# A hybrid RWKV, feed-forward and attention kernel: tanh and u kept in PSUM, two constants as immediates, one step moved to GpSimd, one product saved in every second job, new orders

## The chip, the cores and the metric

The kernel runs on one core of a Trainium2 chip. The metric is the device time of one execution in microseconds. The profile is of one execution on the same core. Five engines work from queues of their own: PE (TensorE), DVE (VectorE), ACT (ScalarE), POOL (GpSimd) and SP (SyncE, which only issues DMAs here). Each takes its instructions strictly in the order in which they were written, and they wait for one another by semaphores.

## The reference, cut to what matters

Input x has 16 sequences of 512 tokens and 128 channels, all in fp32. Four blocks follow: `x + rwkv(norm(x))`, `x + ffn(norm(x))`, `x + attention(norm(x))` and `x + ffn(norm(x))`. The feed-forward quantises its operands blockwise to FP4. The change touches the first block, which has four layers; the part of a layer that matters is:

```
h  = layernorm(x);  hh = h shifted by one token
xk = h*tmk + hh*(1-tmk);  xv = h*tmv + hh*(1-tmv);  xr = h*tmr + hh*(1-tmr)
k, v, sr = xk@Wk, xv@Wv, sigmoid(xr@Wr)
x = x + (sr * wkv(time_decay, time_first, k, v)) @ Wo     # wkv: a scan over tokens
x = x + sigmoid(xr2@Wcr) * (square(relu(xk2@Wck)) @ Wcv)  # after a second layernorm and shift
```

## The kernel before, in words

A job is one layer of one sequence, 64 jobs r = 0 to 63, and each holds [128 channels, 512 tokens] tiles. The 16 sequences stay in SBUF (`X`). The work of a job is cut into some fifty steps, each a small function with an index. Every engine runs a loop over ticks t, and in a tick it issues its steps in an order written out by hand in the source, each for another job: `mul_u(t - 7)` is job t - 7's. So some thirteen jobs are in flight, and the text of the four loops sets the order on each engine. After job 63 the same loops carry 16 feed-forward jobs (`ffn_job`, from tick FFN_AT), 16 attention jobs (`att_job`, from ATT_AT) and 16 more feed-forward jobs (from FFN2_AT); the last steps of one kind run beside the first of the next.

In a recurrent job: norm1 (ACT, L757) and turn1 (PE, four transposes into bank bT) give h, which keep_h1 (ACT) writes to `h1` with the weight and bias of the norm. `sub_dh1` (POOL, L643) forms dh = h - hh. From job 10 on VectorE mixes xk and xr as dh*tm + hh (`mix_t` L307, `mix_rt` L314), and one product each gives k (bank bK) and r (bank bR). v takes two products into bank bV, `W*tmv` on h and `W2 = W*(1-tmv)` on hh (L1092, L1093). VectorE scans the running maximum of k (`scan_pp`), takes d = k - max (`sub_d`) and the capped argument d + time_first (`arg_r`, L337, into `er`). ScalarE forms the exponentials (`args`, `exp_r`, `exp_d`, `exp_k`); VectorE multiplies with v (`mul_rv` L344, `mul_s1` L351) and scans (`scan_bb` L358, `scan_aa` L366). GpSimd adds to the denominator and the numerator (`add_den`, `add_num`). The reciprocal is an approximation: `seeds` (ACT, L841, an exponential of the bits of the denominator), `mul_y` (POOL, L660, one per job), `square_1` (ACT, L848), `mul_u` (DVE, L373) and `rwkv` (DVE, L387); `gated` (DVE, L381) brings in tanh of r (`tanh_r`, ACT, L810) and `scaled_p` (POOL, L666) the seed. `seeds` and `square_1` read their additive constants from a two-column SBUF tile, `seed`. Then output (PE), `add_xa`, the second norm, `sub_dh` (POOL, L673), `mix_k` and `mix_r` (DVE, L404, L411), the four keys (L1135), relu and square (ACT, L867, L874), values (L1152), the gate product (L1142), `tanh_c`, `gate` and `add_xb` (POOL, L678). `rsqrts` (POOL, L601 to L606) takes the roots for the norms of two jobs at once.

The eight PSUM banks are handed from step to step: `bank.hand_over(semaphore, value)` says what ends the new use and returns what ended the last one, which the new user waits for. `lend_T`, `lend_O` and the like do it for a bank that another engine writes first. GpSimd has no access to PSUM in this kernel.

Of the kernel before, what the change touches and what calls it, by code (L numbers as in the profile page):

```python
# [7 lines left out]
I32 = mybir.dt.int32  # L8
ALU = mybir.AluOpType
# [22 lines left out]
FFN_AT = NR + 5  # L32
LN2_LAG = 6
EARLY = 10
GAP = 12
ATT_AT, FFN2_AT, TICKS = FFN_AT + NB, FFN_AT + NB + GAP, FFN_AT + 2 * NB + GAP + 18

# [38 lines left out]
def hybrid_program(nc, x_in, weights, vecs, rows, fp4w, qkv, wout, mask, ident, out):  # L76
    ctx = ExitStack()
    with ctx:
# [9 lines left out]
        class Norm:  # L88
# [30 lines left out]
        seed = sb("seed", [128, 2])  # L119
# [26 lines left out]
        lent_T, lent_O, lent_X, lent_Y, lent_M = {}, {}, {}, {}, {}  # L146
# [20 lines left out]
        consts, ew_done, wneg_done, omt_done, w_mixed, we_done = [sem(k) for k in (  # L167
            "consts", "ew", "wneg", "omt", "w_mixed", "we")]
# [34 lines left out]
        w2_of = lambda r: W2[:, r // NB, :]  # L203
        v_of = lambda r, k: vec[:, k, r // NB:r // NB + 1]
# [13 lines left out]
        def vector():  # L218
# [21 lines left out]
            def prepare_layer(l):  # L240
                wk = lambda k, n=1: W[:, l, k * 128:(k + n) * 128]
                w.wait_ge(w_here[l], 16)
                w.wait_ge(omt_done, 1)
                e.tensor_scalar(W2[:, l, :], wk(WV), omt[:, TMV - TMK, l:l + 1], None, ALU.mult).then_inc(w_mixed, 1)
                e.tensor_scalar(wk(WO), wk(WO), -0.5 * LEAD, None, ALU.mult).then_inc(w_mixed, 1)
                e.tensor_scalar(wk(WCV, 4), wk(WCV, 4), 0.5, None, ALU.mult).then_inc(w_mixed, 1)
                w.wait_ge(w_mixed, W_OPS * l + 1)
                e.tensor_scalar(wk(WV), wk(WV), vec[:, TMV, l:l + 1], None, ALU.mult).then_inc(w_mixed, 1)
                if l == 0:
                    for k, (matrix, mix) in enumerate(((WK, TMK), (WR, TMR))):  # L250
                        e.tensor_scalar(WE[:, 2 * k, :], wk(matrix), vec[:, mix, 0:1], None, ALU.mult)
                        e.tensor_scalar(WE[:, 2 * k + 1, :], wk(matrix), omt[:, mix - TMK, 0:1], None, ALU.mult).then_inc(we_done, 1)
# [79 lines left out]

            def arg_r(r):
                if 0 <= r < NR:
                    w.wait_ge(rwkv_done, r - 1)
                    w.wait_ge(d_done, r + 1)
                    e.tensor_scalar(er[r % 2][:, :], dd[r % 2][:, :], v_of(r, TF), CAP, ALU.add, ALU.min).then_inc(argr_done, 1)  # L337
# [31 lines left out]
            def mul_u(r):  # L369
                if 0 <= r < NR:  # L370
                    w.wait_ge(sq1_done, r + 1)
                    w.wait_ge(ps_done, r + 1)
                    e.scalar_tensor_tensor(out=p[r % 2][:, :], in0=pO[:, :], scalar=CUBIC, in1=p[r % 2][:, :],  # L373
                                           op0=ALU.add, op1=ALU.mult).then_inc(u_done, 1)

            def gated(r):
                if 0 <= r < NR:
                    w.wait_ge(rwkv_done, r - 1)
# [154 lines left out]
            for t in range(TICKS):  # L533
                fh_add(ffn_job(t - 7), 0)
                mix_rt(t - 6)
                mul_up(ffn_job(t - 6), 2)
                fh_sub(ffn_job(t - 7), 0)
                a_inverse(att_job(t - 7))
                arg_r(t - 6)
                weights_rounded(t - Q_AT - 2)  # L540
                fx_scale(ffn_job(t - 3))
                mix_r(t - 11)
                mul_up(ffn_job(t - 6), 3)
                fx_inverse(ffn_job(t - 3))
                init_affine(t - 2)
                mix_k(t - 10)
                fh_max(ffn_job(t - 6))
                fh_add(ffn_job(t - 7), 1)
                prepare(t - 4)
                fh_scale(ffn_job(t - 6))  # L550
                fh_sub(ffn_job(t - 7), 1)
                a_mask(att_job(t - 6), 0)
                gated(t - 7)
                a_max(att_job(t - 6), 0)
                fh_inverse(ffn_job(t - 6))
                mix_t(t - 5)
                weights_scales(t - Q_AT)
# [9 lines left out]
                a_mask(att_job(t - 6), 3)
                scan_aa(t - 6)
                bn1(t - 2)
                a_max(att_job(t - 6), 3)  # L570
                f_bn(ffn_job(t))
                a_bn(att_job(t))
                bn2(t - 8)
                mul_up(ffn_job(t - 5), 0)
                init_stats(t)
                gate(t - 12)
                scan_pp(t - 5)
# [6 lines left out]
                rwkv(t - 7)  # L584

        def gpsimd():
# [139 lines left out]
            for t in range(TICKS):  # L726
                add_num(t - 7)
                sub_dh(t - 10)
                rsqrts(t - 3)
                add_res(ffn_job(t))  # L730
                a_rsqrt(att_job(t - 2))
                fx_scaled(ffn_job(t - 4))
                init_rsqrt(t - 1)
                fx_divided(ffn_job(t - 3))
                scaled_p(t - 7)
                fh_scaled(ffn_job(t - 7), 0)
                mul_y(t - 7)
                add_xb(t - 13)
                weights_scaled(t - Q_AT - 6)
                sub_dh1(t - 4)  # L740
                fh_divided(ffn_job(t - 6), 0)
                fh_scaled(ffn_job(t - 7), 1)
                add_bias(att_job(t - 7))
                add_den(t - 6)
                fh_divided(ffn_job(t - 6), 1)
                f_rsqrt(ffn_job(t - 1))
                weights_divided(t - Q_AT)

        def scalar():
# [236 lines left out]
            for t in range(TICKS):  # L986
                silu(ffn_job(t - 6), 3)
                put_x(ffn_job(t - 9))
                tanh_c(t - 12)
                keep_hq(ffn_job(t - 8), 0)  # L990
                seeds(t - 7)
                fh_magic(ffn_job(t - 7), 1)
                keep_hq(ffn_job(t - 8), 1)
                relu(t - 11, 2)
                a_z(att_job(t - 3))
# [380 lines left out]
```

## Time and profile before

| | us |
|---|---|
| median of 3 runs (lowest, highest) | 1396.85 (1396.33, 1397.9) |
| span of the profiled execution | 1396.8 |
| PE busy | 1311.6 |
| ACT busy | 1261.8 |
| DVE busy | 1250.5 |
| POOL busy | 1160.8 |

The profiled execution's own time is its span, 1396.8 us; nothing stands around it in the table. Busy is the union of the instructions' times; instructions of one engine overlap at their ends, so an engine can look busy throughout and have its instructions start a fixed time apart that is shorter than the duration of each. The start of the next instruction less the start of this one is what it costs in a full queue. TensorE's granted clock is 0.9 or more of full speed in each of the 40 slices.

### The profile page before, as it was taken

What the parts mean: (1) busy time and instruction counts of PE and PEld (TensorE: products, weight loads), DVE (VectorE), ACT (ScalarE), POOL (GpSimd) and SP (SyncE); (2) the same over time, 40 slices, a digit from 0 to 9 for tenths busy, and PEclk for the clock granted to TensorE, in tenths of its full rate; (3) what the DMA queues carried; (4) which work ended last, traced back from release to release, by engine and by line L of the source; (5) the groups of instructions that cost most, each with busy time, mean ns of one, the idle gap of its engine ahead of it and who ended that gap; (6) DMA issues with size and microseconds to landing.
All of it is one profiled execution on the core that took longest, in us unless ns stands there. A gap on an engine that the chain in (4) does not pass through costs nothing.

```text
span 1396.8 us, 23610 instructions
## 1 busy us (share of the span) xinstructions
PE 1311.6 (94%) x7285; PEld 929.9 (67%) x7285; DVE 1250.5 (90%) x2169; ACT 1261.8 (90%) x2533; POOL 1160.8 (83%) x1218
## 2 busy tenths in 40 slices
PE   3699999999999999999999999999999999999997
PEld 1356667666666666676666677766667777667776
DVE  6999999999999999999999999579999467789994
ACT  6799999999999999999999999767777889888874
POOL 6888999999998999998998999969998445467983
PEclk9999999999999999999999999999999999999999
DMA  7000000000000000000000000100000000000011
GB/s 232 0 1 1 1 1 1 1 20 13 1 1 1 1 1 1 1 1 1 1 2 0 1 1 9 31 24 23 24 1 1 1 1 1 1 8 23 24 31 38
DMA packets 26924, 18.55 MB, mean 13 GB/s; under 512 B 1072, under 2 KB 26160, under 8 KB 26800
## 3 DMA queue, kind: packets, MB, share of 16 engines
q1 hardware_dynamic: 26800, 17.05, 4.2%
q8 instruction: 59, 0.97, 0.3%
q14 instruction: 65, 0.53, 0.1%
HBM read 12.85 MB, written 4.19 MB: 12 GB/s over the span
## 4 chain that ended last, share of the span: by engine, by line
ACT 40%; PE 30%; issue 11%; POOL 10%; DVE 8%; DMA 0%; ACTq 0%; SPq 0%; POOLq 0%; DVEq 0%
ACT z L757 10%; ACT kf L867 6%; PE ps L1211 5%; ACT kf L874 3%; PE ps L1190 3%; ACT rc L841 3%; PE ps L1152 3%; ACT ed L818 3%; PE ps L1183 3%; PE ps L1261 3%; PE ps L1135 3%; ACT er L835 2%; PE ps L1243 2%; ACT ed L819 2%; ACT ed L830 2%
## 5 line engine op out<-in xcount | busy, mean ns | idle before, releaser
L1152 PEld LDWEIGHTS ps<-W,kf 128*128 128x128 f32 x2048 | 245.9, 193 | 33.1 <-issue 32.3
L1135 PE MATMUL ps<-xk,W 128*128 128x512 f32 x512 | 262.5, 595 | 1.0 <-DVE xk L404 0.9
L1152 PE MATMUL ps<-W,kf 128*128 128x128 f32 x2048 | 251.2, 276 | 0.0
L757 ACT ACTIVATE z<-X,ln_rs 128x128 f32<-128x128 f32 x512 | 219.2, 720 | 6.1 <-POOL ln_rs L606 6.1
L867 ACT ACTIVATE kf<-ps 128x512 f32<-128x512 f32 x256 | 210.8, 823 | 3.5 <-PE ps L1135 3.5
L874 ACT ACTIVATE kf<-kf 128x1024 f32<-128x1024 f32 x128 | 164.7, 1287 | 0.0
L1040 PEld LDWEIGHTS ps<-idn,z 128*128 128x128 f32 x664 | 81.1, 143 | 113.7 <-issue 68.4
L1040 PE MATMUL ps<-idn,z 128*128 128x128 f32 x664 | 101.9, 277 | 32.8 <-ACT z L757 19.4
L604 POOL TENSOR_TENSOR ln_rs<-ln_rs,mhalf 128x8 f32<-128x8 f32 (+1 forms) x70 | 122.9, 1756 | 0.0
L707 POOL TENSOR_TENSOR W<-W,hsc 128x704 f32<-128x704 f32 x64 | 88.9, 1389 | 30.3 <-DVE hsc L482 30.3
L666 POOL TENSOR_TENSOR p<-p,rc 128x512 f32<-128x512 f32 x64 | 104.2, 1628 | 8.6 <-DVE p L381 8.0
L673 POOL TENSOR_TENSOR dh<-h 128x512 f32<-128x512 f32 x64 | 66.8, 1044 | 48.4 <-ACT h L860 48.2
L1190 PE MATMUL ps<-WU,d 128*128 128x352 f32 x256 | 99.9, 472 | 5.5 <-DVE W L463 4.8
L1183 PE MATMUL ps<-WG,d 128*128 128x352 f32 x256 | 97.6, 463 | 0.6 <-ACT d L898 0.6
L358 DVE TENSOR_TENSOR_SCAN bb<-ps,ed 128x512 f32<-128x512 f32 x64 | 78.3, 1223 | 19.5 <-ACT ed L830 19.4
L713 POOL TENSOR_TENSOR W<-W,hsc 128x704 f32<-128x704 f32 x64 | 88.8, 1388 | 2.6 <-DVE W L494 2.5
L226 DVE BATCH_NORM_STATS2 ln_st<-X 128x6 f32<-128x256 f32 x256 | 90.5, 413 | 0.1
L1122 PEld LDWEIGHTS ps<-W,rc 128*128 128x128 f32 x512 | 67.0, 191 | 33.8 <-issue 33.8
L1142 PEld LDWEIGHTS ps<-W,xc 128*128 128x128 f32 x512 | 64.3, 191 | 36.5 <-ACT sr L810 24.8
L649 POOL TENSOR_TENSOR er<-er,bb 128x512 f32<-128x512 f32 x64 | 81.4, 1273 | 2.3 <-DVE bb L358 2.3
L655 POOL TENSOR_TENSOR rv<-rv,aa 128x512 f32<-128x512 f32 x64 | 81.5, 1273 | 1.4 <-DVE aa L366 1.3
L678 POOL TENSOR_TENSOR X<-X,cr 128x512 f32<-128x512 f32 x64 | 81.5, 1273 | 0.0
(178 smaller groups left out, 4041.5 us busy)
## 6 DMA issues: line engine op xcount, KB each, us to landing
X<-x_in SPq DMA_DIRECT2D x16, 256.0 KB, 6.8
xi<-x_in SPq DMA_DIRECT2D x16, 256.0 KB, 2.8
out<-X SPq DMA_DIRECT2D x16, 256.0 KB, 2.3
W<-weights SPq DMA_DIRECT2D x4, 832.0 KB, 8.4
W<-fp4w SPq DMA_DIRECT2D x1, 560.0 KB, 3.6
row<-rows SPq DMA_DIRECT2D x1, 192.0 KB, 2.9
wqkv<-qkv SPq DMA_DIRECT2D x1, 96.0 KB, 5.9
idn<-ident SPq DMA_DIRECT2D x1, 64.0 KB, 3.0
```

The source lines that it names most:

```text
L226: last = e.bn_stats(g.of(g.st, n)[:, 2 * k:2 * k + 2, :].rearrange("p a s -> p (a s)"), src[:, k * 256:(k + 1) * 256].rearrange("p (a c) - ...
L604: e.tensor_tensor(rs[:, 0, :], rs[:, 2, :], mhalf[:, 0:k], ALU.pow).then_inc(*own.next())
L666: e.tensor_tensor(p[r % 2][:, :], p[r % 2][:, :], rc[r % 2][:, :], ALU.mult).then_inc(ps_done, 1)
L707: e.tensor_tensor(h, h, spread(hsc[n % 2][:, 0, k * 44:(k + 1) * 44], 44), ALU.mult).then_inc(fh_y[k], 1)
L757: last = e.activation(chunk(dst, j), chunk(src, j), ACT.Identity, bias=rs[:, 1, j:j + 1], scale=rs[:, 0, j:j + 1])
L867: e.activation(kf[r % 3][:, f, :], (pF0, pF1)[f % 2][:, :], ACT.Relu).then_inc(relu_done[f], 1)
L874: e.activation(both, both, ACT.Square).then_inc(sq_done[k], 1)
L1040: last = e.transpose(chunk(dst, j), chunk(src, j), idn[:, :])
L1135: e.matmul((pF0, pF1)[f % 2][:, :], w_of(r, WCK + f), xk[r % 2][:, :], start=True, stop=True).then_inc(kf_mm[f], 1)
L1152: last = e.matmul(chunk(pKV, j), kf[r % 3][:, f, j * 128:(j + 1) * 128], w_of(r, WCV + f), start=f == 0 and j == 0, stop=f == 3, skip_grou ...
L1183: e.matmul(pG[j % 2][:, 0:I], chunk(fx[n % 2], j), WG[:, :], start=True, stop=True).then_inc(g_mm, 1)
L1190: e.matmul(pU[j % 2][:, 0:I], chunk(fx[n % 2], j), WU[:, :], start=True, stop=True).then_inc(u_mm, 1)
```

## The change

- `tanh_r` writes its result to PSUM bank bV (over v, after `mul_s1` of that job) and no longer to an SBUF tile; `gated` reads it there. bV is handed to that use by a new `lend_V`. `mul_u` writes its result over bank bO and `rwkv` reads it there; bO stays in use until `rwkv`.
- The additive constants of `seeds` and `square_1` are immediates; the tile `seed` and its two memsets go.
- `arg_r` moves from VectorE to GpSimd, the instruction as it was.
- From layer 1 on (r >= 16), v of an odd job is mixed by VectorE (`mix_v`) and takes one product; of an even job it takes two still, on hh and dh. `big`'s third and fourth quarter hold the mixed tiles. The weights' preparation has one instruction less per layer from layer 1 on. `sub_dh1` and `keep_h1` wait for these uses of dh1 and h1.
- The order of the steps is written anew on all four engines. FFN_AT is NR + 6 (was NR + 5), ATT_AT is 85 as before, FFN2_AT is FFN_AT + 24 (was FFN_AT + 28). On GpSimd a tick's steps stand for earlier jobs than before (its loop runs about two ticks ahead of VectorE's).

```diff
-FFN_AT = NR + 5
-ATT_AT, FFN2_AT, TICKS = FFN_AT + NB, FFN_AT + NB + GAP, FFN_AT + 2 * NB + GAP + 18
+FFN_AT = NR + 6
+ATT_AT, FFN2_AT = FFN_AT + 15, FFN_AT + 24
+xv = [big[:, 2 + k, :] for k in range(2)]
+one_v = lambda r: r >= NB and r % 2 == 1
 def mix_rt(r):
-    w.wait_ge(p_done, r - 2)
+    w.wait_ge(r_mm, r - 2)
+def mix_v(r):
+    if 0 <= r < NR and one_v(r):
+        w.wait_ge(v_mm, r - 1)
+        w.wait_ge(dh1_done, r + 1 - EARLY)
+        e.scalar_tensor_tensor(out=xv[r % 2], in0=dh1[r % 2][:, :], scalar=v_of(r, TMV), in1=h1[r % 3][:, 0:T],
+                               op0=ALU.mult, op1=ALU.add).then_inc(xv_done, 1)
 def arg_r(r):        # moved from vector() to gpsimd()
     w.wait_ge(rwkv_done, r - 1)
     w.wait_ge(d_done, r + 1)
     e.tensor_scalar(er[r % 2][:, :], dd[r % 2][:, :], v_of(r, TF), CAP, ALU.add, ALU.min).then_inc(argr_done, 1)
 def mul_u(r):
-    e.scalar_tensor_tensor(out=p[r % 2][:, :], in0=pO[:, :], scalar=CUBIC, in1=p[r % 2][:, :],
+    e.scalar_tensor_tensor(out=pO[:, :], in0=pO[:, :], scalar=CUBIC, in1=p[r % 2][:, :],
 def gated(r):
-    w.wait_ge(rwkv_done, r - 1)
-    e.scalar_tensor_tensor(out=p[r % 2][:, :], in0=sr[r % 3][:, :], scalar=1.0, in1=rv[r % 2][:, :],
+    w.wait_ge(u_done, r - 1)
+    e.scalar_tensor_tensor(out=p[r % 2][:, :], in0=pV[:, :], scalar=1.0, in1=rv[r % 2][:, :],
 def rwkv(r):
-    e.scalar_tensor_tensor(out=rc[r % 2][:, :], in0=er[r % 2][:, :], scalar=2.0, in1=p[r % 2][:, :],
+    e.scalar_tensor_tensor(out=rc[r % 2][:, :], in0=er[r % 2][:, :], scalar=2.0, in1=pO[:, :],
 def tanh_r(r):
-    w.wait_ge(p_done, r - 2)
-    e.activation(sr[r % 3][:, :], pR[:, :], ACT.Tanh, scale=0.5).then_inc(sr_done, 1)
+    w.wait_ge(*lent_V[r])
+    e.activation(pV[:, :], pR[:, :], ACT.Tanh, scale=0.5).then_inc(sr_done, 1)
 def seeds(r):
-    e.activation(rc[r % 2][:, :], er[r % 2][:, :].bitcast(I32), ACT.Exp, bias=seed[:, 0:1],
+    e.activation(rc[r % 2][:, :], er[r % 2][:, :].bitcast(I32), ACT.Exp, bias=SEED,
 def square_1(r):
-    e.activation(pO[:, :], er[r % 2][:, :], ACT.Square, bias=seed[:, 1:2]).then_inc(sq1_done, 1)
+    e.activation(pO[:, :], er[r % 2][:, :], ACT.Square, bias=-1.0).then_inc(sq1_done, 1)
 def values(r):
+    if r < NB: ...               # as before: W on h1[1:], W2 on h1[:-1]
+    elif one_v(r):
+        w.wait_ge(xv_done, v_mixes(r + 1))
+        e.matmul(pV[:, :], w_of(r, WV), xv[r % 2], start=True, stop=True).then_inc(v_mm, 1)
+    else:
+        e.matmul(pV[:, :], w_of(r, WV), h1[r % 3][:, 0:T], start=True, stop=False)
+        e.matmul(pV[:, :], w2_of(r), dh1[r % 2][:, :], start=False, stop=True).then_inc(v_mm, 1)
+def lend_V(r):
+    lent_V[r] = bV.hand_over(p_done, r + 1)
```

The new orders, recurrent steps alone (other steps, between them, left out):

```
VectorE: scan_aa(t-6) scan_pp(t-5) bn2(t-8) mul_u(t-7) sub_d(t-5) rwkv(t-7) bn1(t-2) gated(t-6) mix_k(t-9)
         mix_t(t-4) mix_r(t-9) mix_rt(t-5) mix_v(t-4) gate(t-11) add_xa(t-7) mul_rv(t-5) mul_s1(t-5) scan_bb(t-5)
GpSimd:  sub_dh(t-11) arg_r(t-7) rsqrts(t-4) sub_dh1(t-5) mul_y(t-8) scaled_p(t-8) add_den(t-7) add_num(t-7)
         add_xb(t-13)
ScalarE: norm2(t-9) relu(t-10,0) square_1(t-7) tanh_r(t-6) square(t-11,1) keep_h2(t-9) relu(t-10,1) relu(t-10,2)
         square(t-10,0) seeds(t-6) args(t-5) keep_h1(t-3) exp_r(t-5) exp_k(t-5) exp_d(t-5) tanh_c(t-10)
         relu(t-10,3) norm1(t-2)
TensorE: turn1(t-4) ff_keys(t-11,3) lend_V(t-7) lend_T(t-6) output(t-8) values(t-6) lend_O(t-7) ff_keys(t-10,0)
         keys(t-5) receptance(t-6) ff_values(t-11,0) ff_keys(t-10,1) turn2(t-9) ff_keys(t-10,2) ff_gate(t-10)
         ff_values(t-11,1)
```

## Rows read from the trace of the kernel before

**Rows 1.** The page, part 1: busy time and share of the span.

```profile
PE 1311.6 (94%) x7285; PEld 929.9 (67%) x7285; DVE 1250.5 (90%) x2169; ACT 1261.8 (90%) x2533; POOL 1160.8 (83%) x1218
```

**Rows 2.** Table of windows (us from the start): length, busy us of each engine, clock, DMA.

```profile
190.00:700.00 510.00, 510.00 (x2783) 349.68 (x2782) 492.80 (x775) 510.00 (x968) 465.14 (x427) 1.00 0.01 3
700.00:780.00 80.00, 75.42 (x416) 52.31 (x415) 79.38 (x123) 76.77 (x146) 72.89 (x64) 1.00 0.00 1
...
850.00:950.00 100.00, 93.10 (x513) 69.47 (x512) 72.17 (x125) 77.14 (x150) 84.02 (x96) 0.93 0.09 25
...
1150.00:1250.00 100.00, 92.40 (x544) 68.23 (x543) 78.97 (x199) 90.49 (x220) 54.25 (x73) 1.00 0.00 1
1250.00:1350.00 100.00, 96.33 (x577) 72.67 (x576) 95.05 (x176) 81.28 (x170) 84.14 (x90) 1.00 0.09 27
```

The columns of rows 2 are PE, PEld, DVE, ACT, POOL, each busy us (and instructions).

**Rows 3.** Windows of single lines: L660, L1227 (two per attention job), L941 (one per feed-forward job).

```profile
318.00:450.00 132.00, 12.74 (x10) 1.00 0.00 1
...
1111.00:1149.40 38.40, 5.11 (x10) 1.90 (x10) 1.00 0.00 1
...
1280.00:1329.50 49.50, 2.99 (x5) 1.00 0.10 29
```

**Rows 4.** Waits of 190 to 700 us: waiter, released by; us, times, longest.

```profile
POOL dh L673 <- ACT h L860: 35.0, 39, 0.9
PEld ps L1142 <- ACT sr L810: 23.9, 39, 0.7
...
DVE bb L358 <- ACT ed L830: 15.5, 38, 0.4
```

**Rows 5.** Timeline of ScalarE: start us, duration us, line, instruction.

```profile
603.30 1.06 ACT L848 ACTIVATE ps<-er,seed 128x512 f32<-128x512 f32 x1
603.91 1.15 ACT L860 ACTIVATE h<-ps,vec 128x512 f32<-128x512 f32 x1
...
606.48 1.10 ACT L841 ACTIVATE rc<-er,seed 128x512 f32<-128x512 int32 x1
607.09 0.97 ACT L867 ACTIVATE kf<-ps 128x512 f32<-128x512 f32 x1
...
609.98 0.97 ACT L825 ACTIVATE ps<-ed 128x512 f32<-128x512 f32 x1
610.52 0.99 ACT L830 ACTIVATE ed<-ed 128x512 f32<-128x512 f32 x1
611.04 1.63 ACT L757 ACTIVATE z<-X,ln_rs 128x128 f32<-128x128 f32 x3
```

**Rows 6.** Timeline of TensorE's matmuls.

```profile
605.20 1.02 PE L1092 MATMUL ps<-h,W 128*128 128x512 f32 x2
606.06 1.02 PE L1093 MATMUL ps<-h,W 128*128 128x512 f32 x2
```

**Rows 7.** Timeline of VectorE.

```profile
606.07 0.74 DVE L387 SCALAR_TENSOR_TENSOR rc<-er,p 128x512 f32<-128x512 f32 x1
606.73 0.74 DVE L314 SCALAR_TENSOR_TENSOR sr<-dh,vec,h 128x512 f32<-128x512 f32 x1
607.39 0.47 DVE L337 TENSOR_SCALAR er<-d,vec 128x512 f32<-128x512 f32 x1
607.79 0.74 DVE L411 SCALAR_TENSOR_TENSOR xc<-dh,vec,h 128x512 f32<-128x512 f32 x1
...
609.72 0.74 DVE L307 SCALAR_TENSOR_TENSOR xt<-dh,vec,h 128x512 f32<-128x512 f32 x1
```

**Rows 8.** Timelines of GpSimd at four places, last the lines' table of 1150 to 1300.

```profile
609.87 1.73 POOL L666 TENSOR_TENSOR p<-p,rc 128x512 f32<-128x512 f32 x1
611.56 1.28 POOL L660 TENSOR_TENSOR er<-er,rc 128x512 f32<-128x512 f32 x1
...
813.00 1.27 POOL L666 TENSOR_TENSOR p<-p,rc 128x512 f32<-128x512 f32 x1
...
872.13 0.62 POOL L602 TENSOR_SCALAR ln_rs<-ln_st 128x4 f32<-128x4 f32 x1
...
888.33 0.23 POOL L602 TENSOR_SCALAR ff_rs<-ff_st 128x4 f32<-128x4 f32 x1
...
L694 POOL TENSOR_TENSOR z<-z,xsc 128x512 f32<-128x512 f32 x7 | 7.4, 1061 | 12.5 <-DVE xsc L442 12.5
```

More of the change, by code:

```diff
@@ L203, in hybrid_program @@
         w2_of = lambda r: W2[:, r // NB, :]
+        xv = [big[:, 2 + k, :] for k in range(2)]
+        one_v = lambda r: r >= NB and r % 2 == 1
+        v_mixes = lambda r: sum(one_v(k) for k in range(r))
         v_of = lambda r, k: vec[:, k, r // NB:r // NB + 1]
@@ L546, in vector @@
[L546 to L550, printed above, removed]
-                fh_sub(ffn_job(t - 7), 1)
[L552 to L557, printed above, removed]
+                fh_inverse(ffn_job(t - 6))
@@ L567, in vector @@
[L567 to L577, printed above, removed]
                 mul_u(t - 7)
                 sub_d(t - 5)
+                rwkv(t - 7)
+                bn1(t - 2)
+                gated(t - 6)
@@ L583, in vector @@
                 fx_sub(ffn_job(t - 3))
-                rwkv(t - 7)
+                mix_t(t - 4)
+                mix_r(t - 9)
+                a_inverse(att_job(t - 6))
+                fh_add(ffn_job(t - 6), 0)
+                mul_up(ffn_job(t - 5), 2)
+                mul_up(ffn_job(t - 5), 3)
+                weights_rounded(t - Q_AT - 3)
+                fh_sub(ffn_job(t - 6), 0)
+                fx_scale(ffn_job(t - 2))
+                a_mask(att_job(t - 5), 0)
+                prepare(t - 1)
+                fh_max(ffn_job(t - 5))
+                mix_rt(t - 5)
+                a_max(att_job(t - 5), 0)
+                fx_inverse(ffn_job(t - 2))
+                mix_v(t - 4)
+                fh_scale(ffn_job(t - 5))
+                gate(t - 11)
+                fh_add(ffn_job(t - 6), 1)
+                add_xa(t - 7)
+                mul_rv(t - 5)
+                mul_s1(t - 5)
+                scan_bb(t - 5)
         def gpsimd():
@@ L726, in gpsimd @@
             for t in range(TICKS):
-                add_num(t - 7)
[L728 to L737, printed above, removed]
-                add_xb(t - 13)
[L739 to L747, printed above, removed]
+                sub_dh(t - 11)
+                fh_divided(ffn_job(t - 8), 0)
+                fh_scaled(ffn_job(t - 9), 1)
+                a_rsqrt(att_job(t - 5))
+                arg_r(t - 7)
+                add_bias(att_job(t - 9))
+                rsqrts(t - 4)
+                add_res(ffn_job(t + 1))
+                init_rsqrt(t - 2)
+                fh_divided(ffn_job(t - 8), 1)
+                weights_scaled(t - Q_AT - 8)
+                f_rsqrt(ffn_job(t - 2))
+                fh_scaled(ffn_job(t - 8), 0)
+                fx_scaled(ffn_job(t - 5))
+                sub_dh1(t - 5)
+                weights_divided(t - Q_AT - 2)
+                mul_y(t - 8)
+                scaled_p(t - 8)
+                fx_divided(ffn_job(t - 4))
+                add_den(t - 7)
+                add_num(t - 7)
+                add_xb(t - 13)
         def scalar():
@@ L986, in scalar @@
             for t in range(TICKS):
[L987 to L995, printed above, removed]
                 silu(ffn_job(t - 5), 0)
-                args(t - 6)
+                keep_x(ffn_job(t - 9))
+                norm2(t - 9)
@@ L1025, in scalar @@
                 keep_h2(t - 9)
-                fx_magic(ffn_job(t - 3))
                 silu(ffn_job(t - 5), 1)
-                square(t - 11, 1)
-                fh_magic(ffn_job(t - 6), 0)
                 keep_fx(ffn_job(t - 4))
                 relu(t - 10, 1)
+                fh_magic(ffn_job(t - 6), 0)
                 silu(ffn_job(t - 5), 2)
+                relu(t - 10, 2)
+                square(t - 10, 0)
+                seeds(t - 6)
+                silu(ffn_job(t - 5), 3)
+                put_x(ffn_job(t - 8))
@@ L1034, in tensor @@
+                f_z(ffn_job(t - 1))
+                args(t - 5)
+                keep_h1(t - 3)
+                exp_r(t - 5)
+                exp_k(t - 5)
+                exp_d(t - 5)
+                a_z(att_job(t - 3))
+                keep_hq(ffn_job(t - 7), 0)
+                tanh_c(t - 10)
+                relu(t - 10, 3)
+                fh_magic(ffn_job(t - 6), 1)
+                norm1(t - 2)
+                keep_hq(ffn_job(t - 7), 1)
         def tensor():
```

194 lines of the change are left out of this document (96 added, 98 removed).

## The prediction

> **What bounds the kernel now.** The page comes first: on the whole span TensorE is busy 94%, and VectorE, ScalarE and GpSimd 90, 90 and 83% [rows 1]. No engine stands out, so I go by stretches. From 190 to 700 us, the recurrent stage with all its steps in flight, the table of windows has TensorE and ScalarE busy 510.0 of 510.0 us, VectorE 492.8, GpSimd 465.1 [rows 2]. Busy time there is a union of overlapping instructions and can hide small gaps, so I look for gaps in two other views. One job takes 13.2 us: the multiplication of L660, one per job, stands ten times in 132 us [rows 3]. The list of waits of that stretch has GpSimd waiting 0.9 us per job for h2, VectorE 0.4 us for the exponential, TensorE's weight loads for the tanh that frees bank bR (0.6 us of a load, of which most is covered by the matmul before it), and no entry for ScalarE at all [rows 4]. So ScalarE, in its written order, is packed for the whole stretch, TensorE is packed but for about 0.1 us, and both others have cover: 13.2 less 12.76 us of busy time on VectorE (492.8 / 38.6 jobs), 13.2 less 12.04 on GpSimd (465.1 / 38.6). An edit pays here only if it takes work from ScalarE, and TensorE has to give the same.
>
> **The change part by part.**
>
> *Two immediates.* In a packed queue the cost of an instruction is the time from its start to the next start. The two activations that read a bias column from `seed` cost 603.91 - 603.30 = 0.61 and 607.09 - 606.48 = 0.61 us; the 512-column exponential without a bias column, with the same kinds of source, costs 610.52 - 609.98 = 0.54 us when it writes PSUM, and the one after it 0.52 when it writes SBUF [rows 5]. I take 0.08 us for each, 0.16 us per job. ScalarE goes to 13.04 us. Bounds: 0 (the immediates cost what the column did) and 0.18.
>
> *Tanh into PSUM.* Same source, other destination. The exponential with an SBUF source costs 0.54 into PSUM and 0.52 into SBUF [rows 5]; I take 0, bounds -0.02 and +0.02 us per job. The wait it adds, on s1 of the job after (bank bV now holds tanh between `mul_s1` and `gated`), stands in ScalarE's queue ahead of square, keep_h2, relu and everything else. `mul_s1` of the next job is third from the end of VectorE's tick and tanh is fourth in ScalarE's next one, so nearly a fifth of a tick lies between, which I count as cover.
>
> *One product for v in every second job.* A 512-column product costs 606.06 - 605.20 = 0.86 us on TensorE, and v takes two of them [rows 6]. Of the jobs from 16 on, 24 save one: 20.6 us of TensorE's work in all, 0.43 us per job on the mean. The other jobs keep about 13.1 us (13.2 less the gap before ff_gate). So TensorE alternates between 13.1 and 12.2 us and stops being a bound. On its own this is worth nothing beyond 0.1 us per job, since ScalarE stands at 13.2; it is the cover under which the immediates count. VectorE pays for it with one mix, 607.39 - 606.73 = 0.66 us in every second job, 0.33 on the mean [rows 7].
>
> *VectorE.* It gives `arg_r` away, 607.79 - 607.39 = 0.40 us. `rwkv`, with both tensors in SBUF, costs 606.73 - 606.07 = 0.66; with one in PSUM I take 0.60, and nothing for `gated` [rows 7]. Sum: 12.76 - 0.40 - 0.06 + 0.33 = 12.63 us (12.96 in a job with the mix, 12.30 in one without). It stays under 13.04.
>
> *GpSimd takes arg_r.* No 512-column tensor_scalar on GpSimd stands in the trace. From below: at 4 columns it is 0.23 us (L602). From above: two full tensors at 512 cost 1.27 (L660). The nearest is the 512-column product with a small spread operand, 1.06 us (L694), and I take 1.04 [rows 8]. Against it stands what VectorE gives back. L666 costs 1.73 us where it starts beside VectorE's mix_t at 609.72 [rows 7], which reads two SBUF tensors, and 1.27 where it does not; L602 at 4 columns costs 0.62 at one place and 0.23 at another [rows 8], so the same instruction stretches there as well. In the new order the four or five mixes follow one another and GpSimd has `rsqrts` (small operands) about there, with scaled_p behind it beside a scan that reads PSUM. I expect L666 to come down by 0.45. Sum: 12.04 + 1.04 - 0.45 = 12.63 us, with the bounds 12.04 + 0.23 - 0.45 = 11.8 and 12.04 + 1.27 + 0.45 = 13.8 (arg_r itself held up beside mix_k, L666 as before). Under 13.04 at my value, over it from arg_r = 1.45 on.
>
> The Trainium skill (GPSIMD Engine Reference, 3.1) gives 769 ns for 512 elements in GpSimd's best one-input loop; with it GpSimd's sum would be 12.36 us. No run here shows it.
>
> *The orders.* I followed each semaphore through the four new lists with the costs above. Every wait is met at 13.04 us per job; the narrowest place is GpSimd's phase: `sub_dh` must start after keep_h2 (about 5.2 us into ScalarE's tick) and end before mix_k at 5.9 us into VectorE's, and its `rsqrts` must be done before norm1. That leaves some 0.5 us. The weight quantisation (its VectorE work stretched the ticks of 700 to 780 us, where ScalarE is busy 76.8 of 80 [rows 2]) is spread wider; I count 1 us gained, between -2 and 3. In the turn to the feed-forward jobs these start one tick later against a shorter recurrent tail; TensorE idles 6.9 of 100 us there now [rows 2]. I count 1 us lost, between 0 and 10 (a whole feed-forward tick). The second feed-forward pass starts 24 ticks after the first, before 28: attention-only ticks of 38.4 / 5 = 7.7 us go, and ticks of attention together with feed-forward come for them and for feed-forward ticks of 49.5 / 5 = 9.9 us [rows 3]. TensorE's work is the same, so only its idle time can be won, 7.6 us of 1150 to 1250 and 3.7 of 1250 to 1350 [rows 2]. I take 2 us won, between 8 lost and 8 won.
>
> *Sum.* 38.6 jobs of 190 to 700 us, the 5 after 780, some 5 before 190 and about half of the gain in the 6 disturbed ones make 52 jobs at 0.16 = 8.3 us. With 1 - 1 + 2 and another 1.2 us for TensorE's relief in the ticks in which it is late (the bounds: 0 and 3) it comes to 11.5 us. The profiled execution's span is 1396.8 us and the median of the runs 1396.85, so the two are taken as one: 1385.3 us.
>
> **The rivals.**
>
> *A, GpSimd becomes the bound and it turns slower.* For it: GpSimd is already the engine whose instructions stretch beside VectorE's two-input ones, and arg_r comes to stand right behind `sub_dh`, on which mix_k waits, so both start together. With arg_r held up by 0.45 and L666 not relieved, a job costs 12.04 + 1.27 + 0.45 = 13.76 on GpSimd; I price it at 13.44 (arg_r at 1.27, nothing given back): + 0.24 x 52 = 12.5, less the 3 us of the other terms: 1406 us. It decides from the point at which GpSimd's job passes 13.2 us. Against it: 0.9 us of idle time per job and the relief of two two-input instructions. Chance 0.13.
> The Trainium skill (SBUF — State Buffer, Terms) says that VectorE and GpSimd arbitrate for a shared port pair that is held for a full instruction while the loser fully blocks. By that rule GpSimd would lose the whole 3.0 us of the mixes; the rows above agree for L666 (0.45 lost beside one mix) and leave it open for L604.
>
> *B, the recurrent stage stays at 13.2 us.* The immediates cost what the column did, or GpSimd lands between 13.1 and 13.2. For it: only the start-to-start times of other functions speak for the 0.08. Then the edges alone remain: 1394 us. Chance 0.15.
>
> *C, the edges give more.* Second pass and turn win what idle time TensorE has, 8 to 10 us more: 1376 us. For it: 11.3 idle us in 1150 to 1350. Against it: a chain inside each job, not order, may make them. Chance 0.14.
>
> My forecast has 0.58.
>
> **How the numbers follow.** The forecast's own range is 1379 to 1391. C and B lie at 1376 and 1394, A at 1406; with half of A inside I reach 1371 to 1403. No change that can be told means within 0.2%, 2.8 us, so 1394.1 to 1399.6: half of B and a little of A, 0.08. Faster: 0.58 + 0.14 + half of B = 0.79. Slower: A and what the turn could lose, 0.13.
>
> **What would show it.** Right: the ten L660s in 127.6 to 130.4 us and no wait of ScalarE; square_1 and seeds at about 0.53 from start to start; TensorE with waits of 0.8 us in every second job; GpSimd at 12.6 busy us per job. Wrong: a wait of ScalarE for arg_r, or of mix_k for dh2 that grows from job to job (A); two activations still at 0.61 (B); the first pass of the feed-forward ending later than 1111 us by more than the recurrent stage won (the turn).

## The result and the profile after

The changed kernel takes 1431.0 us (median of 4 runs, 1429.38 to 1431.37) against 1396.88: a ratio of 1.0236, 95% interval 1.0222 to 1.0249. It is slower by 34 us where 1385.3 was forecast, and lies outside the range. The profiled execution's span is 1429.9 us.

The page's busy line of the changed kernel, and then its windows (PE, PEld, DVE, ACT, POOL as in rows 2):

```profile
PE 1315.8 (92%) x7237; PEld 923.8 (65%) x7237; DVE 1249.0 (87%) x2126; ACT 1266.2 (89%) x2539; POOL 1253.1 (88%) x1280
```

```profile
190.00:700.00 510.00, 489.53 (x2630) 330.90 (x2628) 476.15 (x720) 488.47 (x922) 497.52 (x444) 1.00 0.01 3
...
1345.00:1391.20 46.20, 46.20 (x284) 36.41 (x282) 46.09 (x80) 38.43 (x78) 40.15 (x38) 1.00 0.10 30
```

Against [rows 1] GpSimd has gained 92 us of work, no other engine more than 5. Against [rows 2] ScalarE and TensorE, full before, idle some 20 us in 190 to 700, and GpSimd has gone from 465.1 to 497.5. A job takes 138.4 / 10 = 13.84 us, read as in [rows 3] (the line of `mul_y` is L671 here):

```profile
289.90:428.30 138.40, 12.75 (x10) 1.00 0.03 9
```

The mean over jobs 16 to 48 is 13.84 too. GpSimd starts its `mul_y` alternately 14.03 and 13.65 us apart: the second instruction of the roots (L603) takes 0.63 us beside VectorE's mix of v, which comes in every second job, and 0.25 us without it. One of the longer jobs on GpSimd (start us, duration us), and L603 of the job after it:

```profile
601.53 1.28 POOL L671 TENSOR_TENSOR er<-er,rc 128x512 f32<-128x512 f32 x1
602.76 1.28 POOL L677 TENSOR_TENSOR p<-p,rc 128x512 f32<-128x512 f32 x1
...
607.68 1.08 POOL L684 TENSOR_TENSOR dh<-h 128x512 f32<-128x512 f32 x1
608.86 2.56 POOL L666 TENSOR_SCALAR er<-d,vec 128x512 f32<-128x512 f32 x1
611.49 0.53 POOL L602 TENSOR_SCALAR ln_rs<-ln_st 128x8 f32<-128x8 f32 x1
612.10 0.63 POOL L603 TENSOR_SCALAR ln_rs<-ln_st 128x8 f32<-128x8 f32 x1
612.70 1.66 POOL L605 TENSOR_TENSOR ln_rs<-ln_rs,mhalf 128x8 f32<-128x8 f32 x1
614.44 0.21 POOL L607 TENSOR_TENSOR ln_rs<-ln_rs 128x8 f32<-128x8 f32 x1
...
626.14 0.25 POOL L603 TENSOR_SCALAR ln_rs<-ln_st 128x8 f32<-128x8 f32 x1
```

`arg_r` (L666) costs 611.49 - 608.86 = 2.63 us. `scaled_p` (L677) takes 1.28 where it took 1.73 [rows 8]. There is no gap above 0.1 us; the small ones (ahead of L666 and inside the roots) add up to 0.34 us per job, which with 13.50 us of busy time fills the 13.84. So GpSimd is the full engine. What the others wait for has changed with it, against [rows 4]:

```profile
PEld ps L1056 <- DVE aa L369: 39.9, 35, 1.3
...
DVE xk L407 <- POOL dh L684: 31.5, 37, 0.9
```

```profile
ACT z L769 <- POOL ln_rs L607: 14.3, 37, 0.6
ACT er L850 <- POOL er L666: 7.2, 37, 0.2
```

mix_k waits for GpSimd 0.85 us in every job; GpSimd waited for ScalarE at that place before. ScalarE, which waited for nothing before, now waits for GpSimd's roots and for `arg_r`: 21.5 us, all that it idles in these 510 us.

On ScalarE the two activations with immediates, and tanh with PSUM as its destination:

```profile
604.19 0.58 ACT L863 ACTIVATE ps<-er 128x512 f32<-128x512 f32 x1
604.71 0.55 ACT L825 ACTIVATE ps<-ps 128x512 f32<-128x512 f32 x1
605.18 1.05 ACT L889 ACTIVATE kf<-kf 128x1024 f32<-128x1024 f32 x1
...
608.70 0.64 ACT L856 ACTIVATE rc<-er 128x512 f32<-128x512 int32 x1
609.22 0.73 ACT L833 ACTIVATE ed<-d,ew 128x512 f32<-128x512 f32 x1
```

0.52 us each from start to start (0.61 in [rows 5]), and 0.47 for tanh: the immediates did what they should.

Where the time lies is seen best by stage. The table is worked out from the starts of `mul_y` (job 0 is the first) and `keep_x` (feed-forward job 0 likewise) in the traces, in us:

| | to mul_y(15) | to mul_y(63) | to keep_x(0) | to keep_x(15) | to keep_x(31) |
|---|---|---|---|---|---|
| before | 241.9 | 635.0 | 82.7 | 151.2 | 283.1 |
| after | 255.7 | 666.5 | 79.5 | 151.9 | 273.4 |
| difference | +13.8 | +31.5 | -3.2 | +0.7 | -9.7 |

So the recurrent jobs lost 45 us and everything after them won 12. In the middle of the second feed-forward pass a job takes 46.2 / 5 = 9.24 us with TensorE busy 46.20 of 46.20 us (second window above), where it took 9.9 [rows 3] with VectorE as the full engine:

```profile
1280.00:1329.50 49.50, 48.06 (x283) 35.59 (x283) 49.50 (x91) 42.11 (x87) 45.50 (x51) 1.00 0.10 29
```

But only four jobs took 9.9 in the kernel before. Of the 9.7 us won in the last stage 5.8 lie before keep_x(21), in the stretch with the attention jobs, and 3.9 after it; experiment 7 comes back to this.

### The profile page after: what moved, and what is told of

Same layout as the page of the kernel before. It is cut to its first block, busy times and chain, and to the rows that moved or that the text cites. A ratio compares the mean times of both kernels' runs of the same rounds, so it can differ in the third digit from the quotient of the medians.

```text
span 1429.9 us, 23519 instructions
## 1 busy us (share of the span) xinstructions
PE 1315.8 (92%) x7237; PEld 923.8 (65%) x7237; DVE 1249.0 (87%) x2126; ACT 1266.2 (89%) x2539; POOL 1253.1 (88%) x1280
## 4 chain that ended last, share of the span: by engine, by line
PE 37%; POOL 21%; DVE 17%; ACT 15%; issue 9%; DMA 0%; POOLq 0%; SPq 0%; ACTq 0%; DVEq 0%
ACT z L769 7%; POOL er L666 6%; PE ps L1182 5%; PE ps L1241 5%; PE ps L1165 4%; POOL ln_rs L605 4%; PE ps L1220 3%; PE ps L1213 3%; DVE ln_st L228 3%; PE ps L1056 3%; POOL dh L684 2%; DVE aa L369 2%; PE ps L1229 2%; PE ps L1172 2%; PE ps L1152 2%
## 5 line engine op out<-in xcount | busy, mean ns | idle before, releaser
L1182 PE MATMUL ps<-W,kf 128*128 128x128 f32 x2048 | 256.8, 279 | 0.1
L769 ACT ACTIVATE z<-X,ln_rs 128x128 f32<-128x128 f32 x512 | 204.6, 482 | 35.0 <-POOL ln_rs L607 35.0
L666 POOL TENSOR_SCALAR er<-d,vec 128x512 f32<-128x512 f32 x64 | 157.7, 2463 | 8.7 <-DVE d L340 1.7
L1056 PEld LDWEIGHTS ps<-idn,z 128*128 128x128 f32 x664 | 76.9, 142 | 120.4 <-DVE aa L369 69.3
L882 ACT ACTIVATE kf<-ps 128x512 f32<-128x512 f32 x256 | 143.1, 586 | 3.8 <-PE ps L1165 3.8
L889 ACT ACTIVATE kf<-kf 128x1024 f32<-128x1024 f32 x128 | 135.0, 1055 | 0.0
L605 POOL TENSOR_TENSOR ln_rs<-ln_rs,mhalf 128x8 f32<-128x8 f32 (+1 forms) x70 | 115.0, 1643 | 0.0
L1165 PEld LDWEIGHTS ps<-xk,W 128*128 128x128 f32 x512 | 82.2, 190 | 30.7 <-issue 29.7
L228 DVE BATCH_NORM_STATS2 ln_st<-X 128x6 f32<-128x256 f32 x256 | 95.5, 413 | 0.1
L407 DVE SCALAR_TENSOR_TENSOR xk<-dh,vec,h 128x512 f32<-128x512 f32 x64 | 49.3, 770 | 52.6 <-POOL dh L684 52.6
L1220 PE MATMUL ps<-WU,d 128*128 128x352 f32 x256 | 92.9, 465 | 0.4 <-DVE W L466 0.4
L660 POOL TENSOR_TENSOR rv<-rv,aa 128x512 f32<-128x512 f32 x64 | 82.1, 1283 | 0.0
```

The costliest lines, as they stand in the source:

```text
L228: last = e.bn_stats(g.of(g.st, n)[:, 2 * k:2 * k + 2, :].rearrange("p a s -> p (a s)"), src[:, k * 256:(k + 1) * 256].rearrange("p (a c) - ...
L605: e.tensor_tensor(rs[:, 0, :], rs[:, 2, :], mhalf[:, 0:k], ALU.pow).then_inc(*own.next())
L769: last = e.activation(chunk(dst, j), chunk(src, j), ACT.Identity, bias=rs[:, 1, j:j + 1], scale=rs[:, 0, j:j + 1])
L882: e.activation(kf[r % 3][:, f, :], (pF0, pF1)[f % 2][:, :], ACT.Relu).then_inc(relu_done[f], 1)
L889: e.activation(both, both, ACT.Square).then_inc(sq_done[k], 1)
L1056: last = e.transpose(chunk(dst, j), chunk(src, j), idn[:, :])
```

## The experiments

Each median stands with its ratio to the kernel before, run on the same chip, and the 95% interval.

**1. arg_r back on VectorE, all else as changed.** Named A below.

```diff
 # gpsimd loop
-    arg_r(t - 7)
 # vector loop
     gated(t - 6)
+    arg_r(t - 5)
```

> The changed kernel with arg_r alone put back on VectorE, behind gated in the new order (job t - 5). Theory 1 (GpSimd is the bound, arg_r at 2.64 us from start to start is what fills it): GpSimd falls to about 11.2 us per job, VectorE rises from 12.4 to 12.8, and the job takes ScalarE's sum, 13.0 to 13.1 us instead of 13.87; over some 52 jobs that is 40 to 44 us less than the changed kernel: 1387 to 1391 us. Theory 2 (a chain through the new orders, sub_dh to mix_k to the next wait, sets the pace, whichever engine forms the argument): the job stays at 13.5 us or more, 1412 us or more, and the waits of mix_k for dh2 remain.

1376.1 us, 0.9848 (0.9834 to 0.9863). By stage 243.3, 625.3, 76.9, 151.9, 273.6. A ten-job window of `mul_y` and the table of 190 to 700:

```profile
190.00:700.00 510.00, 507.06 (x2778) 351.34 (x2777) 505.29 (x804) 510.00 (x982) 452.13 (x431) 1.00 0.01 3
```

```profile
300.70:430.90 130.20, 12.75 (x10) 1.00 0.03 10
```

ScalarE is full and a job takes 13.02 us (the mean over jobs 16 to 48 as well), as its sum says. One instruction's engine made 55 us: theory 1 in its mechanism, not in its size, as the time is 11 us below the lower end of what I expected. The recurrent stage before job 15 alone came back by 12.4 us, and my 52 jobs counted only a part of it.

**2. The kernel before with the immediates alone.**

```diff
-    bias=seed[:, 0:1]      # seeds
+    bias=SEED
-    bias=seed[:, 1:2]      # square_1
+    bias=-1.0
```

> The kernel before with the two constants as immediates and nothing else. Theory 1 (ScalarE and TensorE are both full at 13.2): ScalarE has 0.18 us less per job (the two cost 0.52 from start to start in the changed kernel, 0.61 before), TensorE keeps 13.1, so a job takes 13.1 us and the kernel gains at most 0.1 x 52 = 5 us: 1392 to 1395 us. Rival (ScalarE alone is the bound): 0.18 x 52 = 9 us, 1388 us. Rival (TensorE and the handing over of bank bR fix 13.2): no change, 1396 to 1397 us.

1391.35 us, 0.9955 (0.9940 to 0.9970). A job takes 13.10 us: the relief of ScalarE is cut off by TensorE's sum, 0.1 below.

**3. arg_r on GpSimd with one operation.** The time_first goes into the exponential as a bias column; the limit is a column, cap less time_first. The sum is formed in another place, so the output can differ by rounding.

```diff
-    e.tensor_scalar(er, dd, v_of(r, TF), CAP, ALU.add, ALU.min)
+    e.tensor_scalar(er, dd, col(lid, r), None, ALU.min)
-    e.activation(er, er, ACT.Exp)
+    e.activation(er, er, ACT.Exp, bias=v_of(r, TF))
```

> The changed kernel with GpSimd's arg_r cut to one operation: min with a column (cap less time_first, made once), and time_first added by ScalarE as the bias column of the exponential. If GpSimd's cost goes with the number of operations, arg_r costs 1.0 to 1.3 us instead of 2.56 and GpSimd stands at about 12.5 us per job; ScalarE pays 0.09 for the column (13.1): a job at 13.1, 1390 to 1394 us. If the cost is one of tensor_scalar on 512 columns as such, it stays at 2.0 to 2.6 us and the kernel at 1428 to 1434 us. Half way (1.8 us, GpSimd 13.2): 1395 to 1400 us.

1392.96 us, 0.9969 (0.9957 to 0.9982), 13.15 us per job. The instruction takes 1.57 us, half way, but the total lies in the range of the first case. The window of 190 to 700 and VectorE's wait for `sub_dh`:

```profile
190.00:700.00 510.00, 504.26 (x2749) 346.39 (x2748) 497.79 (x756) 509.56 (x971) 500.76 (x466) 1.00 0.01 3
```

```profile
DVE xk L409 <- POOL dh L687: 12.1, 20, 0.6
```

ScalarE is full again, and GpSimd has just come down to it: 500.76 / 38.8 = 12.91 busy us per job and 0.24 us of small gaps make the same 13.15, and mix_k still waits for it in every second job. One operation less was enough, with nothing to spare.

**4. GpSimd's forms by themselves.** Eight instructions ahead of the kernel before; their source is a tile filled for it. Only their durations are read, not the time (one run, 1411.62 us).

> The kernel before with eight GpSimd instructions of 512 columns put ahead of everything, one after the other, while VectorE has next to nothing to do; only their durations are of interest, not the time. Order: tensor_scalar with a column added and a constant minimum (arg_r's form); with two constants, add and min; a column added alone; minimum with a column alone; two constants, mult and add; a constant product alone; arg_r's form on 256 columns; tensor_tensor add with a column spread over 512. Theory 1a (the cost goes by operations): 2.0 us for the two-operation forms and near 1.0 for one, the 256-column one about half of the first. Rival 1b (the minimum has a slow path): forms 1, 2 and 4 near 2.0 and the others near 1.0. Rival 1c (the column operand costs): forms 1, 3 and 4 slow, 2, 5 and 6 fast. tensor_tensor as in the traces, 1.06 to 1.27.

GpSimd's timeline, in the order named there:

```profile
7.11 2.00 POOL L605 TENSOR_SCALAR kf<-kf,vec 128x512 f32<-128x512 f32 x1
9.20 1.92 POOL L606 TENSOR_SCALAR kf<-kf 128x512 f32<-128x512 f32 x1
11.22 1.57 POOL L607 TENSOR_SCALAR kf<-kf,vec 128x512 f32<-128x512 f32 x1
12.89 1.56 POOL L608 TENSOR_SCALAR kf<-kf,vec 128x512 f32<-128x512 f32 x1
14.54 0.63 POOL L609 TENSOR_SCALAR kf<-kf 128x512 f32<-128x512 f32 x1
15.26 1.51 POOL L610 TENSOR_SCALAR kf<-kf 128x512 f32<-128x512 f32 x1
16.87 1.15 POOL L611 TENSOR_SCALAR kf<-kf,vec 128x256 f32<-128x256 f32 x1
18.11 1.04 POOL L612 TENSOR_TENSOR kf<-kf,vec 128x512 f32<-128x512 f32 x1
```

None of the three theories as put. The minimum is no slower than the addition (1.56, 1.57), the column costs 0.05 to 0.1, one operation takes 1.5 and two take 1.9 to 2.0; arg_r's form on 256 columns takes 1.15, so an estimate from its two sizes is 3.3 ns per column and 0.3 us fixed. One form stands apart: two constants, a product and a sum, 0.63 us. That is the form of L601, the only two-operation tensor_scalar that GpSimd has in the kernel before. Adding the same column as a spread tensor (tensor_tensor) takes 1.04 us.

**5. A with two products for v in every job.**

```diff
-one_v = lambda r: r >= NB and r % 2 == 1
+one_v = lambda r: False
```

> The kernel with arg_r on VectorE (1376.1 us, a job 13.02 us from job 15 to 63) with v of every job from two products, mix_v gone. Theory (ScalarE's 13.0 is the bound and TensorE's 13.1 lies just above it): TensorE gets 20.6 us more in all, but a job goes only from 13.02 to 13.11 us, 0.1 x 48 = 5 us: 1380 to 1382 us. Rival (the one product is what won the time; TensorE is late in the disturbed ticks as well): 10 to 20 us, 1386 to 1396 us. Rival (the mix costs VectorE as much as the product gives): 1374 to 1377 us.

1380.75 us, 0.9886 (0.9869 to 0.9902); a job 13.10 us. As the theory has it: the saved product is worth 5 us, not its 20.6.

**6. A with the constants from the tile.** The edit is that of experiment 2, undone.

> The kernel with arg_r on VectorE, with the two constants read from the SBUF tile again. Theory: ScalarE's sum goes up by 2 x 0.09 = 0.18 us, a job from 13.02 to 13.20 us, 0.18 x 52 = 9 us: 1384 to 1386 us. Rival (ScalarE is not the bound in this kernel, the alternation of 12.2 and 13.9 us between jobs comes from VectorE and TensorE): 1376 to 1379 us.

1385.91 us, 0.9915 (0.9898 to 0.9931): + 9.8 us, theory. The immediates are worth more here than in experiment 2, because TensorE has been relieved.

**7. A with the second pass four ticks later.**

```diff
-ATT_AT, FFN2_AT = FFN_AT + 15, FFN_AT + 24
+ATT_AT, FFN2_AT = FFN_AT + 15, FFN_AT + 28
```

> The kernel with arg_r on VectorE, with the second feed-forward pass 28 ticks behind the first again, not 24. Theory (the closer start is what won about 10 us between the 16th and the last feed-forward job, 283.1 us in the kernel before, 273.6 here): 1384 to 1387 us. Rival (the new order inside the feed-forward ticks won it, 9.2 us per job instead of 9.9, and the closer start gave nothing): 1375 to 1379 us.

1377.1 us, 0.9852 (0.9838 to 0.9867), and keep_x(15) to keep_x(31) still 272.7 us. So the closer start won nothing, as the rival has it. But the rival's account of the 10.4 us against the kernel before (9.2 us a job for 9.9) is not what the trace shows: with the old start four feed-forward jobs of the second pass go at 9.89 us in the new orders too, VectorE busy 39.20 of 39.40 us. The 9.24 us in the changed kernel belong to the closer start, which puts more of the pass beside the attention jobs and wins nothing in sum. Of the 10.4 us, 6.5 come from the first three intervals of the pass (keep_x 13.49, 9.26 and 9.89 us apart; 16.93, 12.80 and 9.41 before), where it still meets the last attention jobs, 1.9 from two near its end, 0.8 from the stretch before its first keep_x and 1.1 from the eight intervals between. The new orders are the likely cause; the attention jobs also follow the first pass by 15 ticks here and by 16 before, and no run separates the two.

**8. A with tanh and u in SBUF, and tanh alone in SBUF.**

```diff
-    tanh_r: out=pV         gated: in0=pV           # both experiments
+    tanh_r: out=sr[r % 3]  gated: in0=sr[r % 3]
-    mul_u: out=pO          rwkv: in1=pO            # the first alone
+    mul_u: out=p[r % 2]    rwkv: in1=p[r % 2]
# cut: the waits and the handing over of bV and bO, as in the kernel before
```

> The kernel with arg_r on VectorE, with tanh and u written to SBUF tiles again and bV and bO handed over as in the kernel before. Theory (the move to PSUM takes 0.07 us from rwkv and otherwise frees GpSimd's reads beside it, none of which is on the bound): 1376 to 1378 us. Rival (VectorE, at 12.8 us per job and 13.2 in jobs with the mix, is a bound in every second job): 0.07 to 0.15 us per job, 1379 to 1384 us. Rival (holding bV and bO longer cost something): 1372 to 1375 us.

> The kernel with arg_r on VectorE (1376.1 us) with tanh alone in SBUF again; u stays in PSUM. With both back it took 1409.9 us, and there rwkv (both inputs in SBUF) took 1.44 us beside GpSimd's sub_dh instead of 0.67, while gated took its 0.67. Theory (a VectorE instruction with two SBUF inputs waits until the GpSimd instruction in flight is done, and rwkv is the one that meets one): u in PSUM is what counts, 1375 to 1379 us. Rival (bank bV's hand over or tanh's waits made the 34 us): 1400 to 1410 us.

Both in SBUF: 1409.94 us, 1.0090 (1.0075 to 1.0105), none of the three. Tanh alone: 1376.03 us, 0.9854 (0.9840 to 0.9869). So with tanh in SBUF, u's place makes all 34 us (u alone in SBUF was not run; bank bO is also handed over earlier with u in SBUF, which sets TensorE and ScalarE free sooner, not later). Where, is seen when VectorE's and GpSimd's timelines of the first are laid side by side:

```profile
604.93 0.67 DVE L382 SCALAR_TENSOR_TENSOR p<-ps,p 128x512 f32<-128x512 f32 x1
605.52 0.68 DVE L340 TENSOR_TENSOR d<-ps,pp 128x512 f32<-128x512 f32 x1
606.12 1.44 DVE L396 SCALAR_TENSOR_TENSOR rc<-er,p 128x512 f32<-128x512 f32 x1
607.49 0.75 DVE L228 BATCH_NORM_STATS2 ln_st<-X 128x6 f32<-128x256 f32 x2
```

```profile
605.96 1.05 POOL L685 TENSOR_TENSOR dh<-h 128x512 f32<-128x512 f32 x1
608.49 0.40 POOL L609 TENSOR_SCALAR ln_rs<-ln_st 128x8 f32<-128x8 f32 x1 [1.47 <-DVE ln_st L228]
```

`rwkv` (L396) with both tensors in SBUF begins at 606.12 beside GpSimd's L685, which ends at 607.01, and is done 0.55 us after that. With u in PSUM the median of that line is 0.67 us, here 1.43. With tanh alone in SBUF `gated` has two SBUF inputs, and in every second job it meets the same GpSimd instruction and stretches to 1.02 us likewise. That costs no time (1376.03 against 1376.1), though it uses up what VectorE had left: it is busy 509.43 of 510.00 us then, and ScalarE 509.42. One of these places:

```profile
600.74 1.00 DVE L390 SCALAR_TENSOR_TENSOR p<-sr,rv 128x512 f32<-128x512 f32 x1
```

```profile
600.16 1.04 POOL L685 TENSOR_TENSOR dh<-h 128x512 f32<-128x512 f32 x1 [0.82 <-ACT h L875]
```

In the first version VectorE becomes the full engine (510.00 of 510.00 us of 190 to 700) at 13.6 us a job, and GpSimd's roots come to wait for the statistics behind it. The Trainium skill (SBUF — State Buffer, Terms) has VectorE and GpSimd share a port pair that one of them holds for a full instruction while the other waits; here the trace agrees, for these two instructions (but see the last section).

**9. The kernel before, arg_r alone moved to GpSimd.**

```diff
 # gpsimd loop
     sub_dh(t - 10)
+    arg_r(t - 6)
```

> The kernel before, in its own orders, with arg_r alone moved to GpSimd, behind sub_dh (same job as before). Theory (the instruction's own 2.0 to 2.6 us is the whole cost, in whatever order): GpSimd's starts add up to 12.2 + 2.1 to 2.6 = 14.3 to 14.8 us per job instead of 13.2, over 52 jobs 57 to 83 us: 1454 to 1480 us. Rival (the new orders made it dear, by putting it beside the mixes): GpSimd hides most of it in its 0.9 us of idle time per job, below 1430 us.

1477.68 us, 1.0584 (1.0568 to 1.0600), 14.39 us a job, at the upper end of the theory. That the number fits is partly luck: the instruction takes 2.43 us, but it also waits 0.65 for rwkv of two jobs before, and `scaled_p` comes down to 1.27 us here as well, neither of which the theory had:

```profile
L654 POOL TENSOR_SCALAR er<-d,vec 128x512 f32<-128x512 f32 x28 | 68.1, 2432 | 18.3 <-DVE rc L381 18.3
```

The new orders did not make it dear: they took the 81 us that it costs in the old ones down to the 55 of experiment 1.

**10. The kernel before, tanh and u alone moved to PSUM.** The edit of experiment 8 the other way round, with `lend_V(t - 7)` ahead of `values(t - 6)`.

> The kernel before, in its own orders, with tanh and u in PSUM and nothing else. Theory (the old orders have no room for tanh in bV: values of the next job starts there at 618.4 us, gated reads at 622.3): TensorE's queue stands at values until gated is done, a job takes 14 to 16 us and the kernel 1440 to 1540 us. Rival (the phases of the engines shift and swallow it): 1395 to 1402 us. Rival (rwkv's relief shows at once): 1390 to 1395 us.

1749.96 us, 1.2538 (1.2517 to 1.2559), 18.8 us a job, beyond the theory's upper end, by its mechanism and one turn more. Waits of 300 to 700 us:

```profile
DVE rv L344 <- ACT er L835: 109.3, 21, 5.5
ACT h L803 <- PE ps L1041: 107.3, 21, 5.4
PEld ps L1093 <- DVE p L381: 83.6, 21, 4.0
PE ps L1093 <- DVE p L381: 66.3, 21, 3.2
```

TensorE stands at values for gated; turn1, behind it in TensorE's queue, is late for keep_h1; exp_r, behind that in ScalarE's, is late for mul_rv; and gated comes after that in the next tick. A ring through three queues (TensorE, ScalarE, VectorE), not a sum of one engine. The granted clock is 0.87 in that stretch, in which TensorE is busy 333.7 of 400 us; before it was 1.00.

**11. A with all feed-forward and attention jobs one tick earlier.**

```diff
-FFN_AT = NR + 6
+FFN_AT = NR + 5
```

> The kernel with arg_r on VectorE, all feed-forward and attention jobs one tick earlier (FFN_AT = NR + 5, as before). Theory (the turn's idle time shrinks by part of a tick): 1370 to 1376 us. Rival (TensorE's work is the same there, and a recurrent tick just gets longer): 1375 to 1378 us. Rival (a wait on the last recurrent jobs stops a queue): 1380 us or more.

1383.26 us, 0.9907 (0.9892 to 0.9921): 7 us slower than A. Of the profile's 7.4 us to the last keep_x, 3.7 lie before job 63, 2.6 between it and keep_x(0), and 1.7 after keep_x(15). The time lies in the range of the third case; whether its mechanism is at work has not been followed further. The planned tick was the better one.

## Why the prediction was wrong, point by point

- *What bounds the kernel.* Right: ScalarE full, TensorE 0.1 us below. With ScalarE relieved alone a job takes TensorE's 13.10 us (experiment 2, and experiment 5 in the new orders), and with TensorE relieved alone ScalarE's 13.20 (experiment 6).
- *Two immediates.* Right, 0.09 each against 0.08. Worth 6 us alone and 9.8 with TensorE relieved.
- *One product.* Right: cover, not a gain. 5 us, with 20.6 taken from TensorE.
- *GpSimd takes arg_r.* This step failed, and with it the sign. I took 1.04 us and gave 1.27 as the upper end; it costs 2.00 us alone (experiment 4), 2.56 beside VectorE's mixes. The upper end was no bound. The 0.23 us of L602 at 4 columns says nothing of the cost per column, and two-tensor instructions at 1.27 don't bound a tensor_scalar, which takes 1.5 us for one operation; why GpSimd is slower on one tensor than on two is not shown. The 769 ns for 512 elements that the Trainium skill (GPSIMD Engine Reference, 3.1) gives as a best case points the same way: here forms with one tensor take 1.5 to 2.0 us, all but the product and sum of two constants with 0.63.
- *The sum for GpSimd* had a second fault. Its base of 12.04 us is busy time; from start to start GpSimd's job before was 13.20 less 0.91 of waiting, 12.29 us, as small gaps of under 0.1 us fill 0.26. With them arg_r had room for about 1.2 us under ScalarE's 13.04, not 1.45.
- *L666 comes down by 0.45.* Right (1.73 to 1.27), and more: the pow went from 1.85 to 1.66, the last of the roots from 0.39 to 0.21 and their second instruction from 0.62 to 0.44 on the mean. With 0.26 us of gaps and the measured price my sum gives 12.63 + 0.26 - 1.04 + 2.63 = 14.5 us; these three take off some 0.6, and 13.84 is measured.
- *Rival A* had the engine, the place and its signs (mix_k waits for dh2, ScalarE for arg_r), with a chance of 0.13. Of its way there, half held: arg_r was held up (by 0.56 us), but L666 was relieved in full, and the largest part, the instruction's own price of 2.00 us, was in no rival. Its 13.44 us doesn't follow from its terms either: 12.04 + 1.27 is 13.31, which would be 1400 us and not 1406. That 13.44 lies nearer to the 13.84 measured is luck. 0.4 us more in 52 jobs are 21 of the 25 us between 1406 and 1431. The chance was too small, because an instruction that the trace never shows was the only new load on an engine with 0.4 us to spare by my own sum.
- *Tanh and u in PSUM.* I gave the move 0.06 us of rwkv. In the new orders, with arg_r on VectorE, it holds 34 us (experiment 8), as otherwise rwkv would meet GpSimd's sub_dh each time; and the old orders have no room for it as they stand (experiment 10). I would have seen the first, had I asked of each two-input instruction of VectorE what runs on GpSimd beside it.
- *The orders.* ScalarE waits for nothing at 13.02 us a job in A, as I had walked them (`mul_s1` is last but one in VectorE's tick, not third from the end, which changes nothing here). The turn cost nothing (3.2 us won). The last stage won 9.7 us against my 2, and not by the closer start as I argued (experiment 7). What in the orders does it was not isolated.
- *The first 15 jobs* were in the sum in part only: 13.8 us were lost there in the change, 12.4 of them by arg_r.

A and the version with tanh alone in SBUF are the fastest of all, 1376.1 and 1376.0 us, 1.5% under the kernel before.

## What to carry to other kernels

Before work is moved to an engine that is to stay under a full one, its price there has to come from the same instruction, operands and size; if no row shows it, it is measured first (eight instructions in one run told it here), and it is the first rival until then. A saved constant or product counts only down to the next engine's sum, so two such edits are priced together. Of each instruction with two SBUF tensors on VectorE, ask which GpSimd instruction runs beside it: one input in PSUM saved 0.76 us of an instruction here, where I had priced 0.06.

## What the runs showed of the hardware

- GpSimd's tensor_scalar on 128x512 fp32: 1.5 us with one operation, 1.9 to 2.0 with two, but 0.63 for a product and a sum with two constants (experiment 4).
- VectorE and GpSimd hold each other up both ways: rwkv 0.67 to 1.43 us; in the changed kernel mix_t takes 1.10 us for 0.74 while arg_r runs beside it:

```profile
608.87 0.75 DVE L407 SCALAR_TENSOR_TENSOR xk<-dh,vec,h 128x512 f32<-128x512 f32 x1 [0.91 <-POOL dh L684]
609.54 1.10 DVE L309 SCALAR_TENSOR_TENSOR xt<-dh,vec,h 128x512 f32<-128x512 f32 x1
610.56 0.74 DVE L414 SCALAR_TENSOR_TENSOR xc<-dh,vec,h 128x512 f32<-128x512 f32 x1
```

  But not for a full instruction: arg_r (608.86 to 611.42) runs beside 2.5 us of mixes and loses 0.56 us, and of them only mix_t is stretched. The rule of the Trainium skill (SBUF — State Buffer, Terms) fits rwkv and gated in experiment 8 and not this.
- A VectorE instruction with one input in PSUM and one in SBUF costs 0.59 us from start to start (L382 in experiment 8), with both in SBUF and a column 0.66 (L314 in [rows 7]), at 512 fp32 columns.
